# A perceiver block: routed experts with split down products, and one accumulator that the scatters add to one after the other

## The chip, the cores and the metric

One core of one Trainium2 chip runs the whole program. The metric is the device time of one execution in microseconds (us), the median of several runs.

## What is computed

The input has 8 x 64 = 512 tokens of 512 features. Three blocks follow, each added to its input: cross attention to a context, gated chunk attention with 16 heads, and a mixture of experts. The change touches the last one:

```python
def _moe(xf, gate_w, w1, w2, w3):
    ...
    h = silu(einsum('ecd,edi->eci', xb, w1)) * einsum('ecd,edi->eci', xb, w3)
    ob = einsum('eci,eid->ecd', h, w2)
    y_pairs = ob[buf_idx] * w_s[:, None]
    y = zeros((T, D)).at[t_s].add(y_pairs)          # T = 512 tokens, D = 512
shared = silu(xf @ sw1) * (xf @ sw3) @ sw2
x = x + (y + shared)                                # xf is the layer norm of x
```

Each token goes to 6 of 32 experts (inner width 352 = 128 + 128 + 96); the shared expert, twice as wide, sees all tokens. All arrays are fp32.

## The kernel before

The program is written engine by engine, with a semaphore for every dependency; nothing is scheduled by a tool. Each engine's block (`@block.sync`, `gpsimd`, `scalar`, `vector`, `tensor`) is executed in the order of its lines, and a waiting instruction holds everything behind it on its engine. SP issues the loads and stores, POOL (GpSimd) the indirect DMAs.

**Split products.** Where a product has to be exact but cheap, an fp32 matrix is cut in two fp32r halves: ScalarE copies it to the high half (`..._h`, `..._hi`), VectorE subtracts that to get the low half (`..._l`, `..._lo`), and TensorE makes three products (`mm3`, L316: high x high, high x low, low x high). What is not split is multiplied as plain fp32 in one instruction.

**Items.** A router on the chip sorts the token-expert pairs into items of up to 128 pairs of one expert. Item m has its list of tokens in a column of `tl` and its routing weights in `wl`. Its number decides the buffers: k = m % 2 for `xe`, `h`, `hT`, `ob`, and the PSUM banks. Turn i of the loops handles items 2i and 2i + 1. The eight steps of the shared expert (NSH = 8) run before item 0 and use the same functions.

**What each engine does in the turn of item m.**
- TensorE (`ex_pe`, L1024): transposes of item m + 1's tokens; the up products of item m (`ex_up`, 24 fp32r products of 352 columns, L318 to L320); the down product of item m - 1 (`ex_down`, L970, three fp32 products of 512 columns, L978); the transposes of item m's h (`ex_hT`, L963).
- ScalarE (`ex_act`, L1036): hT of item m - 1 out of PSUM (L1006, L1007), the high half of item m + 1's tokens (L1011), silu (L996), the high halves of item m + 1's w1 and w3 (`ex_act_w13`, L985, w_h<-w_raw, L988).
- VectorE (`ex_dve`, L1070): the low half of the tokens (L1015), copies of the token numbers for the next gather (`take`) and scatter (`give`), `ob` = down product x routing weight of item m - 2 (`ex_dve_ob`, L1053, L1061), h (L1001), the low halves of item m + 1's w1 and w3 (w_l<-w_raw,w_h, L992).
- POOL (`ex_pool`, L1108): the gather of item m + 3's tokens (L1094), then the scatter of item m - 2 (`ex_scatter`, L1097, L1098), which adds 128 rows of 2 KB to an accumulator in device memory. There are two accumulators, `y_scratch0` for even and `y_scratch1` for odd items, both zeroed early (L1251), so that two scatters in flight never touch the same bytes. `ob[k]` and `give[k]` are written again only when the scatter before it from the same k has landed (`acc_done[k]`, L1057).
- SP: the weights of an expert, once per expert (`cond=new`), up to four experts ahead, into four slots of `w13_raw` and `w2_raw` (`ex_load_w13`, L1139, waits for `w13_ready`; `ex_load_w2`, L1151, waits for `d_ps`).

**Slots of the halves.** w13_h and w13_l have two slots. The conversion for item m + 1 always goes to slot 1 - k. If item m is the second item of its expert, its up products read the slot of item m - 1, row `SLOT` of the list, and that is the slot which the conversion is about to overwrite; `ODD` then delays the conversion until item m's up products have ended:

```python
e.wait_ge(h3_ps, m + odd + NSH)
ex_act_w13(e, 1 - k, 0, i + (k + 2), raw)
```

**The end.** The last two items (34 and 35) are not scattered. TensorE multiplies `ob` with a one-hot matrix `home` (token x row) into PSUM, fp32 (L2087); SP reads both accumulators back, 1 MB each (L1315, L1317), each once the last scatter into it has landed; VectorE adds the first, the second and the PSUM banks to x, four tiles each (L1888, L1892, L1896), and SP stores tile by tile (L1320).

Of the kernel before, what the change touches and what calls it, by code (L numbers as in the profile page):

```python
# [24 lines left out]
ALU = mybir.AluOpType  # L25
ACT = mybir.ActivationFunctionType
AX = mybir.AxisListType
# [11 lines left out]
def perceiver_block(nc, x_in, ctx_in, ctxT_in, Wq, Wk, WkT, Wv, Wo, gq, gk,  # L39
# [17 lines left out]
    with stack:  # L57
# [129 lines left out]
        xe = sbuf(moe, "xe", [P, 2, D])  # L187
# [5 lines left out]
        ob = sbuf(moe, "ob", [P, 2, D])  # L193
# [4 lines left out]
        gateT = sbuf(moe, "gateT", [E, T])  # L198
# [5 lines left out]
        hots = sbuf(moe, "hots", [P, 2, TT * TOP_K * E])  # L204
        hot = hots[:, 0, :].rearrange("p (t k n) -> p t k n", t=TT, k=TOP_K)
        hotp = hots[:, 1, :].rearrange("p (t k n) -> p t k n", t=TT, k=TOP_K)
        home = hots[:, :, 0:T]
# [24 lines left out]
        EXPERT, LOADED, SLOT, ODD, FIRST, HELD = range(6)  # L232
        lst_f = sbuf(moe, "lst_f", [1, 6, ML + 1])
        lst_j = sbuf(moe, "lst_j", [1, ML + 1])
        lst = sbuf(moe, "lst", [1, 6, ML + 1], I32)
# [9 lines left out]
        y_back = [xn_c, w2_and_lists[:, 4 * W2:4 * W2 + TT * D].rearrange("p (t d) -> p t d", t=TT)]  # L245
# [4 lines left out]
        y_dram = [nc.dram_tensor(f"y_scratch{k}", [T + P, D], F32) for k in range(2)]  # L250
# [5 lines left out]
        ctxT_arrived = [sem(f"ctxT_arrived{g}") for g in range(5)]  # L256
# [14 lines left out]
        IO_RK, IO_SPARE, IO_TOKENS = 32, 80, 96  # L271
# [31 lines left out]
        y0_in, y1_in = sem("y0_in"), sem("y1_in")  # L303
        y_sum, out_ready, home_ready, last_ps = sem("y_sum"), sem("out_ready"), sem("home_ready"), sem("last_ps")
# [7 lines left out]
        hT_ps, hT_ready, d_ps = sem("hT_ps"), sem("hT_ready"), sem("d_ps")  # L312

# [286 lines left out]
        def xa_dve_scores(e, i, j):  # L600
# [9 lines left out]
            e.tensor_reduce(nmx[:, 0, bb], sc[:, bb, :], AX.X, ALU.max, negate=True).then_inc(mx_ready, 1)  # L610
            e.wait_ge(mx_ready, i * 4 + (j + 1))
            e.tensor_tensor(nmx[:, 1, bb], nmx[:, 0, bb], rq[:, bb], ALU.mult).then_inc(nmx_ready, 1)

        def xa_dve_norm(e, i, j):
            bb = slice(2 * j, 2 * j + 2)
            e.wait_ge(p_ready, i * 4 + (j + 1))
            e.reciprocal(rsm[:, bb], sm[:, bb]).then_inc(rsm_ready, 1)
            e.wait_ge(rsm_ready, i * 4 + (j + 1))
# [8 lines left out]
        def xa_dve_rq(e, p):  # L627
            e.wait_ge(rms_ready, p + 1)
            e.reciprocal(rq[:, :], rms[:, :]).then_inc(rq_ready, 1)
# [333 lines left out]
        def ex_hT(e, k, u):  # L963
            e.wait_ge(h_ready, u + 1)
            e.wait_ge(hT_ready, u)
# [4 lines left out]
        def ex_down(e, k, u, w, landed, bank_free=None):  # L970
# [8 lines left out]
            m.then_inc(d_ps, 1)  # L979

# [27 lines left out]

        def ex_act_xT(e, m, k):
# [14 lines left out]
        def ex_pe(e, i, k, first=False, last=False):  # L1024
# [6 lines left out]
            ex_up(lambda c: xeT_h[:, k, c, :], lambda c: xeT_l[:, k, c, :], k, item_value(e, SLOT, m), m * 2 + 6)  # L1031
            ex_down(e, 1 - k, m + (NSH - 1), 1 if first else item_value(e, FIRST, m - 1, 3),
# [3 lines left out]
        def ex_act(e, i, k, last=False):  # L1036
# [3 lines left out]
            if last:  # L1040
                ex_act_silu(e, k, m + NSH)
                return
# [1100 lines left out]
```

## Time and profile before

| | |
|---|---|
| median of 3 runs | 1017.85 us (1016.35 to 1021.34) |
| the profiled execution | 1024.46 us, its span 1022.7 us |
| busy in the span | TensorE 97%, its weight loads 81%, VectorE 65%, ScalarE 53%, POOL 24% |
| first up product of item 0 / of item 35 | 735.7 us / 999.9 us into the span |
| DMA | 144.03 MB, mean 141 GB/s over the span |

The span runs from the first to the last instruction of the core; the execution's own time holds what lies around it too. The rows further down are from the same profiled execution. Matmuls overlap: their pace is read from start to start, not from the duration of one.

### The profile page before, as it was taken

How to read it: one execution, taken by the hardware profiler on the slowest of the kernel's cores; microseconds unless marked ns; L12 is line 12 of the kernel's file. 1: busy time of each engine (PE TensorE's matmuls, PEld its weight loads, DVE VectorE, ACT ScalarE, POOL GpSimd, SP SyncE). 2: the span in 40 equal slices, each digit the busy share in tenths (PEclk: the TensorE clock that was granted, in tenths of full speed). 3: DMA queues.
4: the chain of work that ended last, by engine and by line, in shares of the span. 5: the costliest groups of instructions: out<-in, count | busy, mean ns of one | idle time of the engine just before them, and what ended most of it. 6: DMA issues, size and time to landing. Idle time of an engine off the chain costs nothing.

```text
span 1022.7 us, 18723 instructions
## 1 busy us (share of the span) xinstructions
PE 993.1 (97%) x5468; PEld 828.9 (81%) x5469; DVE 669.1 (65%) x1022; ACT 541.0 (53%) x894; POOL 246.4 (24%) x170
## 2 busy tenths in 40 slices
PE   8899899999999999999999999989999999999997
PEld 7788698889898987888888888777777777777874
DVE  5655655675567665667787675667566677666765
ACT  6444575657566666554555543541356555545551
POOL 2200221323032152223333300010123343334331
PEclk9899999999999998999999999999999999999999
DMA  9100353321331331122221106211678889998995
GB/s 312 48 0 1 82 201 104 103 58 45 102 103 51 85 114 63 61 83 82 82 82 62 41 21 232 63 42 49 232 206 267 268 284 310 345 313 283 282 323 149
DMA packets 75567, 144.03 MB, mean 141 GB/s; under 512 B 13476, under 2 KB 40996, under 8 KB 75280
## 3 DMA queue, kind: packets, MB, share of 16 engines
q1 hardware_dynamic: 67680, 131.48, 38.4%
q0 software_dynamic: 7856, 12.16, 5.7%
q8 instruction: 17, 0.28, 0.1%
q14 instruction: 14, 0.11, 0.0%
HBM read 146.86 MB, written 14.02 MB: 157 GB/s over the span
## 4 chain that ended last, share of the span: by engine, by line
PE 74%; SPq 6%; DMA 6%; DVE 6%; issue 5%; ACT 4%; DVEq 0%; ACTq 0%
PE ps L318 19%; PE ps L319 18%; PE ps L320 18%; PE ps L710 6%; PE ps L978 6%; DMA w_raw<-in_w 4%; SPq L945 2%; PE ps L777 1%; PE ps L787 1%; SPq L1119 1%; PE ps L767 1%; DMA wo_raw<-in_owT 1%; DVE w_l L992 1%; ACT wo_h L406 1%; PE ps L697 1%
## 5 line engine op out<-in xcount | busy, mean ns | idle before, releaser
L992 DVE TENSOR_TENSOR w_l<-w_raw,w_h 128x1408 fp32r<-128x1408 f32 x76 | 121.8, 1625 | 37.9 <-ACT w_h L988 25.8
L988 ACT ACTIVATE w_h<-w_raw 128x1408 fp32r (+1 forms) x76 | 102.6, 1373 | 54.7 <-DMA w_raw<-in_w 39.2
L978 PE MATMUL ps<-w_and_lists,hT 128*128 (+3 forms) x264 | 121.5, 596 | 0.0
L739 POOL TENSOR_TENSOR lw_l<-lw_raw,lw_h 128x1024 fp32r<-128x1024 f32 x32 | 77.0, 2411 | 145.8 <-ACT lw_h L735 140.5
L318 PE MATMUL ps<-w_h,xeT_h 128*128 x288 | 97.4, 338 | 5.4 <-DVE w_l L992 4.6
L319 PE MATMUL ps<-w_l,xeT_h 128*128 x288 | 93.1, 323 | 0.0
L320 PE MATMUL ps<-w_h,xeT_l 128*128 x288 | 93.0, 323 | 0.0
L1094 POOL DMA_INDIRECT xe<-xn_scratch,take x37 | 39.4, 1066 | 220.1 <-DVE ob L1061 148.3
L978 PEld LDWEIGHTS ps<-w_and_lists,hT 128*128 128x128 f32 (+1 forms) x264 | 47.9, 189 | 44.0 <-issue 43.0
L318 PE MATMUL ps<-xT_hi,lw_h 128*128 128x512 f32 x192 | 78.3, 408 | 0.0
L319 PE MATMUL ps<-xT_lo,lw_h 128*128 128x512 f32 x192 | 77.3, 403 | 0.0
L320 PE MATMUL ps<-xT_hi,lw_l 128*128 128x512 f32 x192 | 76.4, 398 | 0.0
L1564 DVE TENSOR_REDUCE ssk<-sqk 128x4 f32<-128x512 f32 (+1 forms) x64 | 43.6, 685 | 36.8 <-ACT sqk L1409 36.6
L1409 ACT ACTIVATE sqk<-ps 128x512 f32<-128x512 f32 x64 | 38.1, 597 | 47.2 <-PE ps L320 42.2
L318 PEld LDWEIGHTS ps<-w_h,xeT_h 128*128 128x128 f32 x288 | 54.4, 189 | 10.4 <-issue 10.1
L710 PE MATMUL ps<-pT,ctx 128*128 128x128 f32 x512 | 62.1, 277 | 0.6 <-ACT pT L582 0.3
L710 PEld LDWEIGHTS ps<-pT,ctx 128*128 128x128 f32 x512 | 59.1, 192 | 2.2 <-ACT pT L582 2.2
L1098 POOL DMA_INDIRECT y_scratch<-ob,give x34 | 55.5, 1631 | 21.4 <-DVE ob L1061 11.6
L592 POOL TENSOR_TENSOR wq_l<-wq_raw,wq_h 128x1024 fp32r<-128x1024 f32 x8 | 19.3, 2410 | 170.0 <-ACT wq_h L552 170.0
L883 DVE RECIPROCAL q_r<-q_r 128x512 f32<-128x512 f32 x16 | 53.6, 3347 | 6.0 <-ACT q_r L859 6.0
L318 PE MATMUL ps<-wk_h,cT_h 128*128 128x512 f32 (+1 forms) x128 | 52.2, 408 | 4.3 <-DVE ssk L1564 2.6
L319 PEld LDWEIGHTS ps<-w_l,xeT_h 128*128 128x128 f32 x288 | 54.2, 188 | 0.0
(315 smaller groups left out, 2543.8 us busy)
## 6 DMA issues: line engine op xcount, KB each, us to landing
w_raw<-in_w SPq DMA_DIRECT2D x78, 704.0 KB
w_and_lists<-in_w SPq DMA_DIRECT2D x39, 512.0 KB
w_and_lists<-in_w SPq DMA_DIRECT2D x39, 192.0 KB
rkB<-rk_scratch SPq DMA_DIRECT2D x56, 128.0 KB, 3.2
wq_raw<-in_Wq SPq DMA_DIRECT2D x8, 512.0 KB, 4.6
wo_raw<-in_Wo SPq DMA_DIRECT2D x16, 256.0 KB, 2.8
lw_raw<-in_kwT SPq DMA_DIRECT2D x8, 512.0 KB, 3.3
lw_raw<-in_qwT SPq DMA_DIRECT2D x8, 512.0 KB, 3.4
```

The costliest lines, as they stand in the source:

```text
L318: nc.tensor.matmul(out_ap, lh, rh, start=first, stop=False)
L319: nc.tensor.matmul(out_ap, lh, rl, start=False, stop=False)
L320: return nc.tensor.matmul(out_ap, ll, rh, start=False, stop=last)
L710: m = e.matmul(ps[:, 4 + j % 2, at:at + P], ctx[:, b * KPB + t, hcol(c)], pT[:, b, t, :], start=t == 0, stop=t == KPB - 1)
L739: e.tensor_tensor(lw_l[n][:, :, :], lw_raw[n][:, :, :], lw_h[n][:, :, :], ALU.subtract).then_inc(lw_ready[n], 1)
L883: e.reciprocal(q_r[:, k, :], q_r[:, k, :]).then_inc(q_recip, 1)
L978: m = e.matmul(ps[:, 6 + k, :], hT[r, k, c, :], w2_raw[r, slot(w), c, :], start=c == 0, stop=c == FC - 1)
L988: e.activation(w13_h[:, k, n, :, :], w13_raw[:, slot(raw), n, :, :], ACT.Copy).then_inc(w13_hi_s, 1)
L992: e.tensor_tensor(w13_l[:, k, n, :, :], w13_raw[:, slot(raw), n, :, :], w13_h[:, k, n, :, :], ALU.subtract).then_inc(w13_ready, 1)
L1094: e.indirect_dma_start(xe[:, k, :], None, xn_dram.ap(), bass.IndirectOffsetOnAxis(ap=take[:, k:k + 1], axis=0), bounds_check=T - 1, oob_is ...
L1098: e.indirect_dma_start(y_dram[k].ap(), bass.IndirectOffsetOnAxis(ap=give[:, k:k + 1], axis=0), ob[:, k, :], None, bounds_check=T - 1, oob_ ...
L1564: e.tensor_reduce(ssk[:, t, bass.ds(g * 4, 4)], sqk[:, t % 2, :].rearrange("p (h n) -> p h n", n=P), AX.X, ALU.add).then_inc(sqk_free, 1)
```

## The change

Five edits, four in the routed experts and one in the way their results are added up. The items stay the same, in the same order.

1. The down product of a routed item: its two whole chunks of 128 are split into halves, hT (`hT_h`, `hT_l`) and w2 (into `xT_hi`, `xT_lo`, which are free by then); six fp32r products take the place of two fp32 ones, the third chunk of 96 stays fp32. The shared expert's down stays as it was.
2. `ob` is written by ScalarE instead of VectorE.
3. Each item uses its own slot k of w13_h and w13_l; `SLOT` and `ODD` are gone, and the conversion waits for h3_ps of item m - 1 in all cases.
4. At the end, `home` and `ob` are fp32r (`ob_h`, `ob_l`), two products for each tile and item in the place of one.
5. One accumulator `y_scratch`. It isn't zeroed: SP writes x with the shared expert's part into it (waiting for d_read = 8), so that the last step adds only the read-back and PSUM, tile by tile. POOL holds each scatter until the one of the item before has landed, and the first until x has.

Core of the diff (names of buffers, semaphore renames and the attention's `soft_step`, which replaces three semaphores by one in the same places, are left out):

```diff
+        def ex_down_halves(e, m, k, w):
+            e.wait_ge(hT_ready, m * 2 + (NSH + 2))
+            e.wait_ge(d_read, m + (NSH - 1))
+            e.wait_ge(w2_ready, m + 1)
+            for c in range(FC - 1):
+                mm3(ps[:, 6 + k, :], hT_h[:, k, c, :], hT_l[:, k, c, :], xT_hi[:, 2 * k + c, :], xT_lo[:, 2 * k + c, :],
+                    c == 0, False)
+            r = slice(0, FW[-1])
+            e.matmul(ps[:, 6 + k, :], hT[r, k, FC - 1, :], w2_raw[r, slot(w), FC - 1, :], start=False, stop=True).then_inc(d_ps, 1)
...
+        def ex_dve_hT_low(e, m, k):
+            e.wait_ge(hT_ready, m * 2 + (NSH + 1))
+            e.tensor_tensor(hT_l[:, k, :, :].rearrange("p c n -> p (c n)"), ps[:, 5, 0:(FC - 1) * P],
+                            hT_h[:, k, :, :].rearrange("p c n -> p (c n)"), ALU.subtract).then_inc(hT_ready, 1)
+
+        def ex_act_w2(e, i, k, raw):
+            e.wait_ge(w2_in[k], i * 32 + 64)
+            e.activation(xT_hi[:, 2 * k:2 * k + 2, :], w2_raw[:, slot(raw), 0:FC - 1, :], ACT.Copy).then_inc(w2_hi_s, 1)
+
+        def ex_dve_w2(e, m, k, raw):
+            e.wait_ge(w2_hi_s, m + 1)
+            e.tensor_tensor(xT_lo[:, 2 * k:2 * k + 2, :], w2_raw[:, slot(raw), 0:FC - 1, :], xT_hi[:, 2 * k:2 * k + 2, :],
+                            ALU.subtract).then_inc(w2_ready, 1)
+
+        def ex_act_ob(e, i, k, out=ob):
+            m = i * 2 + k
+            if not isinstance(i, int) or i > 0:
+                e.wait_ge(acc_done[k], i * 16)
+            e.wait_ge(d_ps, m + (NSH + 1))
+            e.activation(out[:, k, :], ps[:, 6 + k, :], ACT.Copy, scale=wl[:, bass.ds(m, 1)]).then_inc(d_read, 1)
...
-            e.wait_ge(h3_ps, m + odd + NSH)
-            ex_act_w13(e, 1 - k, 0, i + (k + 2), raw)
-            ex_act_w13(e, 1 - k, 1, i + (k + 2), raw)
...
+            if not last and (not isinstance(m, int) or m > 0):
+                e.wait_ge(h3_ps, m + NSH)
+                ex_act_w13(e, 1 - k, 0, i + (k + 2), raw)
+                ex_act_w13(e, 1 - k, 1, i + (k + 2), raw)
+            ex_act_w2(e, i, k, own)
...
         def ex_scatter(e, k):
-            e.indirect_dma_start(y_dram[k].ap(), bass.IndirectOffsetOnAxis(ap=give[:, k:k + 1], axis=0), ob[:, k, :], None,
+            e.indirect_dma_start(y_dram.ap(), bass.IndirectOffsetOnAxis(ap=give[:, k:k + 1], axis=0), ob[:, k, :], None,
                                  bounds_check=T - 1, oob_is_err=False, compute_op=ALU.add).then_inc(acc_done[k], 16)
...
             e.wait_ge(d_read, i * 2 + (k + NSH + 1))
             e.sem_inc(acc_turn, 1)
+            if not isinstance(i, int) or i * 2 + k > 0:
+                e.wait_ge(acc_done[1 - k], i * 16 + k * 16)
+                e.sem_inc(acc_turn, 1)
             ex_scatter(e, k)
...
-            for k in range(2):
-                e.dma_start(y_dram[k].ap().rearrange("(t p) d -> p t d", p=P),
-                            zeros[:, :].unsqueeze(1).to_broadcast([P, TT + 1, D])).then_inc(scratch_io, 16)
...
-            for m in (2, 3, 4):
+            for m in (2, 3):
                 ex_load_w13(e, m, m % 2, m // 2 + 1, values[m])
             for m in (1, 2, 3):
                 ex_load_w2(e, m, m % 2, m // 2 + 1, values[m])
+            ex_load_w13(e, 4, 0, 3, values[4])
+            e.wait_ge(d_read, NSH)
+            e.dma_start(y_dram.ap()[0:T, :].rearrange("(t p) d -> p t d", p=P), x[:, :, :]).then_inc(scratch_io, 16)
...
             for m in range(4):
+                if m == 2:
+                    e.wait_ge(scratch_io, IO_X)
                 ex_pool(e, m // 2, m % 2)
...
-                return e.matmul(ps[:, t, :], home[:, k, t * P:(t + 1) * P], ob[:, k, :], start=k == 0, stop=k == 1)
+                one = home[:, k, t * P:(t + 1) * P]
+                e.matmul(ps[:, t, :], one, ob_h[:, k, :], start=k == 0, stop=False)
+                return e.matmul(ps[:, t, :], one, ob_l[:, k, :], start=False, stop=k == 1)
```

The order of three engines in the loop body, as the built programs have it (the changed program's lines are shifted, L327 is `mm3`'s first product there, L318 here).

TensorE, the down product of the item before, between the last up product and the transposes of h. Before:

```order
L978 ISA
L978 MATMUL ps<-w_and_lists,hT 128x512
L964 REGISTER_ALU
L967 MATMUL ps<-ident,h 128x128 x2
L967 MATMUL ps<-ident,h 96x128
```

and changed, where the first three products stand twice:

```order
L327 MATMUL ps<-xT_hi,hT_h 128x512
L328 MATMUL ps<-xT_lo,hT_h 128x512
L329 MATMUL ps<-xT_hi,hT_l 128x512
L999 ISA
L999 MATMUL ps<-w_and_lists,hT 128x512
L973 REGISTER_ALU
L976 MATMUL ps<-ident,h 128x128 x2
L976 MATMUL ps<-ident,h 96x128
```

L978 stands three times before; now it is L999, once, behind six products on halves. The place in the order is the same.

VectorE, one item from h to the next h. Before (the second item of a turn):

```order
L1001 TENSOR_TENSOR h<-h,ps 128x352
L992 TENSOR_TENSOR w_l<-w_raw,w_h 128x1408
L1015 TENSOR_TENSOR xeT_l<-ps,xeT_h 128x512
L1091 COPY take<-tl 128x1
L1059 COPY give<-tl 128x1
L1061 TENSOR_SCALAR ob<-ps,wl 128x512
```

and changed:

```order
L1021 TENSOR_TENSOR h<-h,ps 128x352
L1012 TENSOR_TENSOR w_l<-w_raw,w_h 128x1408
L1048 TENSOR_TENSOR xT_lo<-w_and_lists,xT_hi 128x1024
L1038 TENSOR_TENSOR hT_l<-ps,hT_h 128x256
L1065 TENSOR_TENSOR xeT_l<-ps,xeT_h 128x512
L1165 COPY take<-tl 128x1
L1116 COPY give<-tl 128x1
```

The product for w_l stands twice in both. Two low halves have come in behind it, ob has gone to ScalarE, where it stands between xeT_h and silu; w2's high half stands there behind the two of w_h.

POOL, the first item of a turn of the loop, with what each waits for. Before:

```order
L1112 REGISTER_ALU [waits xeT_ps]
L1094 DMA xe<-xn_scratch,take 128x512 [waits take_ready]
L1104 REGISTER_ALU [waits give_ready]
L1098 DMA y_scratch<-ob,give 640x512 [waits d_read]
```

and changed:

```order
L1189 REGISTER_ALU [waits xeT_ps]
L1168 DMA xe<-xn_scratch,take 128x512 [waits take_ready]
L1178 REGISTER_ALU [waits give_ready]
L1181 REGISTER_ALU [waits d_read]
L1172 DMA y_scratch<-ob,give 640x512 [waits acc_done1]
```

The order of gather and scatter is the same; the scatter has one wait more, for the landing of the scatter from the other slot.

## Rows read from the trace of the kernel before

**Rows 1.** Windows of the items; columns in the first row.

```profile
core 0: us, PE busy (x) PEld busy (x) DVE busy (x) ACT busy (x) POOL busy (x), PEclk, DMA share, GB/s
735.70:832.20 96.50, 95.53 (x482) 75.82 (x482) 63.36 (x88) 51.45 (x75) 33.16 (x25) 1.00 0.81 250
832.20:883.90 51.70, 51.45 (x261) 40.62 (x261) 35.66 (x49) 29.14 (x42) 19.43 (x15) 1.00 1.00 325
883.90:924.60 40.70, 38.33 (x189) 29.04 (x187) 25.76 (x35) 21.30 (x32) 13.19 (x10) 1.00 0.92 303
924.60:999.90 75.30, 73.56 (x368) 57.55 (x367) 51.67 (x70) 41.70 (x60) 25.30 (x19) 1.00 0.93 299
```

**Rows 2.** Timeline of PE over one item: start us, us, engine line op.

```profile
865.80 2.74 PE L978 MATMUL ps<-w_and_lists,hT 128*128 x6
868.38 0.50 PE L967 MATMUL ps<-ident,h 128*128 128x128 f32 x3
...
869.12 0.41 PE L318 MATMUL ps<-w_h,xeT_h 128*128 x1
...
876.35 0.41 PE L318 MATMUL ps<-w_h,xeT_h 128*128 x1
```

**Rows 3.** Timeline of PE in the attention stage, fp32r products of 512 columns.

```profile
599.97 0.39 PE L318 MATMUL ps<-xT_hi,lw_h 128*128 128x512 f32 x1
600.20 0.40 PE L319 MATMUL ps<-xT_lo,lw_h 128*128 128x512 f32 x1
```

**Rows 4.** Waits, 760 to 1000 us: us in total, times, longest.

```profile
ACT w_h L988 <- DMA w_raw<-in_w: 39.2, 30, 2.3
```

**Rows 5.** Groups by form, whole span: busy us, mean ns of one, idle before.

```profile
L1061 DVE TENSOR_SCALAR ob<-ps,wl 128x512 f32<-128x512 f32 x36 | 26.7, 742 | 6.5 <-PE ps L978 6.5
...
L1560 DVE TENSOR_TENSOR cT_l<-ctxT,cT_h 128x1024 fp32r<-128x1024 f32 x3 | 3.7, 1226 | 1.1 <-ACT cT_h L1399 1.1
...
L449 DVE TENSOR_TENSOR ao_l<-ps,ao_h 128x256 fp32r<-128x256 f32 x4 | 1.7, 414 | 0.4 <-ACT ao_h L444 0.4
...
L735 ACT ACTIVATE lw_h<-lw_raw 128x1024 fp32r<-128x1024 f32 x32 | 33.6, 1052 | 10.8 <-PE ps L320 10.8
...
L1011 ACT ACTIVATE xeT_h<-ps 128x512 fp32r<-128x512 f32 x36 | 21.5, 596 | 22.3 <-issue 20.6 <-PE ps L1021 1.7
```

**Rows 6.** Timeline of VectorE between two items.

```profile
866.08 0.52 DVE L1001 TENSOR_TENSOR h<-h,ps 128x352 f32<-128x352 f32 x1 [1.07 <-PE ps L320]
...
867.02 1.63 DVE L992 TENSOR_TENSOR w_l<-w_raw,w_h 128x1408 fp32r<-128x1408 f32 x1 [0.42 <-issue]
...
868.96 1.63 DVE L992 TENSOR_TENSOR w_l<-w_raw,w_h 128x1408 fp32r<-128x1408 f32 x1 [0.32 <-ACT w_h L988]
```

**Rows 7.** Timeline of POOL, a gather and the scatter behind it.

```profile
865.14 1.05 POOL L1094 DMA_INDIRECT xe<-xn_scratch,take  x1 [4.55 <-DVE ob L1061]
...
866.49 1.59 POOL L1098 DMA_INDIRECT y_scratch<-ob,give  x1 [0.30 <-issue]
```

**Rows 8.** Software queue, windows 870:872.2, 872.2:873.8, 873.8:875.4: packets, MB, engines' share.

```profile
q0 software_dynamic: 95, 0.17, 30.6%
...
q0 software_dynamic: 69, 0.11, 36.3%
...
q0 software_dynamic: 28, 0.04, 12.8%
```

**Rows 9.** Timeline from item 34's down product to the end.

```profile
1004.03 2.84 PE L978 MATMUL ps<-w_and_lists,hT 128*128 x6
...
1004.18 1.55 POOL L1098 DMA_INDIRECT y_scratch<-ob,give  x1 [5.60 <-DVE ob L1061]
...
1008.93 0.40 SPq L1317 DMA_DIRECT2D w_and_lists<-y_scratch  x1
...
1011.63 6.17 PE L2087 MATMUL ps<-ob,hots 128*128 128x512 f32 x14
...
1017.49 2.47 DVE L1896 TENSOR_TENSOR x<-x,ps 128x512 f32<-128x512 f32 x4
```

More of the change, by code:

```diff
@@ L197, in perceiver_block @@
         gw_l = sbuf(moe, "gw_l", [P, DC, E], F32R)
-        gateT = sbuf(moe, "gateT", [E, T])
+        with ExitStack() as router_rows:
+            gateT = sbuf(router_rows, "gateT", [E, T])
+        hT_l = sbuf(moe, "hT_l", [P, 2, FC - 1, P], F32R)
         gate = sbuf(moe, "gate", [P, TT, E])
@@ L1068, in ex_dve_x, with homes, ex_dve_ob_low, ex_dve @@
             e.tensor_tensor(x[:, u % TT, :], x[:, u % TT, :], ps[:, 6 + u % 2, :], ALU.add).then_inc(d_read, 1)
[L1070 removed]
+        def homes(e, i):
+            e.wait_ge(pool_consts, 10)
+            for k in range(2):
+                e.tensor_scalar(home[:, k, :], iota_t[:, :], tl_f[:, 1, bass.ds(i * 2 + k, 1)], None,
+                                ALU.is_equal).then_inc(home_ready, 1)
+        def ex_dve_ob_low(e, i, k):
+            m = i * 2 + k
+            e.wait_ge(d_read, m + (NSH + 1))
+            e.scalar_tensor_tensor(ob_l[:, k, :], ps[:, 6 + k, :], wl[:, bass.ds(m, 1)], ob_h[:, k, :], ALU.mult,
+                                   ALU.subtract).then_inc(home_ready, 1)
+        def ex_dve(e, i, k, own, ahead=None, last=False):
             m = i * 2 + k
             if last:
[L1074 to L1078 removed]
+                ex_dve_give(e, ahead, k)
+            if not isinstance(m, int) or m > 0:
+                ex_dve_hT_low(e, m - 1, 1 - k)
+            if last:
+                homes(e, i)
+            if not last:
+                ex_dve_xT(e, m + 1, 1 - k)
+                ex_dve_take(e, m + 3, 1 - k)
             if isinstance(i, int) and i == 0:
                 ex_dve_x(e, NSH - 2 + k)
[L1081 to L1082 removed]
+            elif not last:
+                ex_dve_give(e, i - 1 if ahead is None else ahead, k)
             ex_dve_h(e, k, m + NSH)
[L1084 to L1085 removed]
+            raw = None if last else raw_slot(e, m + 1)
+            if not last and (not isinstance(m, int) or m > 0):
                 ex_dve_w13(e, 1 - k, 0, m * 2 + 7, raw)
                 ex_dve_w13(e, 1 - k, 1, m * 2 + 8, raw)
+            ex_dve_w2(e, m, k, own)
+            return raw
         def ex_dve_take(e, m, k):
@@ L1545, in _ @@
             ex_act_xT(e, 0, 0)
-            ex_act(e, 0, 0)
-            ex_act(e, 0, 1)
-            with e.Fori(1, last_act) as i:
-                ex_act(e, i, 0)
-                ex_act(e, i, 1)
-            ex_act(e, last_act, 0)
-            ex_act(e, last_act, 1, last=True)
-            ex_act_hT(e, 1, last_act * 2 + (NSH + 1))
+            raw = ex_act(e, 0, 0, 0)
+            raw = ex_act(e, 0, 1, raw)
+            raw = ex_act(e, 1, 0, raw)
+            ex_act(e, 1, 1, raw)
+            with e.Fori(2, last_act) as i:
+                raw = ex_act(e, i, 0, raw_slot(e, i * 2))
+                ex_act(e, i, 1, raw)
+            ahead_act = turn_ahead(e)
+            raw = ex_act(e, last_act, 0, raw_slot(e, last_act * 2), ahead_act)
+            ex_act(e, last_act, 1, raw, ahead_act, last=True)
+            ex_act_hT_halves(e, last_act * 2 + 1, 1)
+            for k in range(2):
+                ex_act_ob(e, last_act, k, ob_h)
         @block.vector
```

169 lines of the change are left out of this document (81 added, 88 removed).

## The prediction

> **What bounds the kernel now.** The change touches the last quarter: 36 items of up to 128 tokens each, for 32 experts. I read the windows first [rows 1], cut where items 0, 13, 20, 25 and 35 start their first product (13, 7, 5 and 10 periods). The reader is to see two things. TensorE is busy for 258.87 of 264.2 us, so it looks like the bound, at the granted clock 1.00 (2.4 GHz) throughout. But the DMA share is 0.81, then 1.00, 0.92, 0.93. The periods are 96.5/13 = 7.42, 51.7/7 = 7.39, 40.7/5 = 8.14 and 75.3/10 = 7.53 us. The PE timeline [rows 2] gives TensorE's own period: 869.12 to 876.35 = 7.24 us, of which the down projection takes 865.80 to 868.38 = 2.58 us and the two groups of transposes 0.74, so the up products take the other 3.9. A new expert brings 2 x 128 x 1408 x 4 + 128 x 1024 x 4 + 96 x 512 x 4 bytes = 2.16 MB, gather and scatter 0.52 MB more. At the 325 GB/s of the second window 2.69 MB take 8.3 us. So the stage is bound by TensorE while it has loads in hand, and by the DMA once these are used up: the third window is such a stretch. The waits say the same: ScalarE waits 39.2 us in all, in 30 pieces, for w_raw to land [rows 4].
>
> **Down projection in halves.** Today three fp32 products run as six passes, 0.43 us apart (2.58/6). Two of the three become three fp32r products each; these follow one another at 0.23 us for 512 columns [rows 3]. New: 6 x 0.23 + 0.86 = 2.24 us, a gain of 0.34 per item, 11.6 us over the 34 downs that run before item 35's up products end. The Trainium skill (FP8 and Floating Point Precision, section TensorE Precision Notes) says that true FP32 makes four passes: four of 0.23 would be 0.92 per chunk, the gain 0.46 per item and 15.6 in all. The trace has 0.86, and the sum goes by it.
>
> **Its price on the other engines.** VectorE gets a low half of 128x1024 (1.23) and one of 128x256 (0.41) and loses ob (0.74): +0.90. ScalarE gets a high half of 128x1024 (1.05) and ob (about 0.60, like xeT_h from PSUM): +1.65 [rows 5]. In the second window VectorE is busy 35.66/7 = 5.09 per item and ScalarE 29.14/7 = 4.16, so 6.0 and 5.8 of a period of 6.9: nothing as sums. The tight spot is the handover [rows 6]: h at 866.08, w_l from 867.02, done at 868.65. TensorE starts the next item at 869.12 and would want it at 868.78. The second w_l ends at 870.59, and TensorE wants it half of the up products (1.9 us) after its start, at 870.7. Both still fit, by 0.1 us; I take nothing, with 0.1 to 0.3 us per item as the bad end (up to 10 us).
>
> **Own slot for each item.** The second item of an expert no longer makes the next conversion wait for h3_ps + odd. Four experts have two items (36 against 32); a late conversion shows as a period of about 7.59 instead of 7.24, so 0.35 each, 1.4 at most, about 1.0 where the DMA isn't behind.
>
> **What the DMA takes back.** In the first window the DMA share is 0.81, so the gain can show: 13 x 0.34 + 1.0 = 5.4. Over the other 22 periods a faster TensorE only asks sooner. The room there is the idle share, 0.08 x 40.7 + 0.07 x 75.3 = 8.5 us, while TensorE would offer 7.1. Since the stalls come earlier once the reserve is drained faster, I take little of it: 1.5, between 0 and 7.1.
>
> **x into the accumulator.** SP now waits for d_read = 8 (the shared half of all tiles is in x), then writes 1 MB, ahead of item 5's weights; behind that wait stand the loads of items 5 and up. The load of item 4 moves behind three w2 loads. 1.05 MB at 325 GB/s is 3.2 us, in the least loaded window: between 0 and 3.2, I take 1. The two writes of zeros go; they lie far ahead, beside attention: nothing. Three one-partition list steps go: I take nothing.
>
> **The chained scatters.** POOL now issues a scatter only when the one before has landed; behind the wait stands the next gather, and ScalarE's ob and VectorE's give wait for the scatter two back. The trace of before shows no such wait, so I bound the landing. The last scatter, alone, starts at 1004.18, and SP, which waits for it, issues at 1008.93: 4.75 us [rows 9]. The one at 866.49 [rows 7] shares the DMA with weights: the software queue carries 30.6% until 872.2, 36.3% until 873.8, 12.8% until 875.4 [rows 8], which I read as gather first, scatter behind it, landed by 875.4: 8.9 us. The next scatter starts one period (7.24) later, 1.7 us before that. So the wait is real wherever weights stream. But the 8.9 us hold the gather's transfer, issued 1.35 us ahead of it (865.14): a scatter held back while the gather runs has less in front of it. From one landing to the next the queue then needs about the 7 us that it needs today. I expect POOL to slip some 2 us behind, once, and then keep the pace; each ob slot has a whole period to spare. Cost: 0 to 12, I take 1.
>
> **The tail.** From item 34's down (1004.03) to the end (1022.7) are 18.7 us [rows 9]. New, from the start of that down: 2.24 + 0.34; item 35's hT split on ScalarE and VectorE, about 1.35; its down 2.24 (6.2). The four products of k = 0 take 8 x 0.23 = 1.84 beside the split of ob, so k = 1 runs from 8.1, a tile each 0.46; 14 passes take 6.17 us today. Of the additions four remain instead of twelve. The last result would be ready at about 10.8, and from the end of today's last additions (1017.49 + 2.47 = 1019.96) to the end of the span are 2.7: 13.5 us. The other branch is the read-back, 1 MB now, not 2: scatter 33 must first see scatter 32 land. If it starts where it starts today and lands 4.75 later, the four reads come at about +10.5, and the end at +14. Gain 4.5, between 2 and 5.2.
>
> **Sum.** -5.4 - 1.5 + 1 + 1 - 4.5 = -9.4, rounded with the three list steps to -9.9. The profiled execution took 1024.46 us (span 1022.7), 0.65% above the median 1017.85 of the runs shown; the difference of 9.9 goes on the median: 1008 us.
>
> **The rivals.**
> DMA takes it all in the loop: the second window with its share of 1.00 speaks for it, the 0.81 of the first against it. Only the tail stays, less the x write: 1014.
> TensorE's pace holds throughout (all room of the DMA is used): 11.6 + 1.4 + 5.2 = 18: 1000. The third window speaks against it.
> The chain of scatters becomes the bound. If a scatter beside weights needs 8.9 us from its start even with nothing of its queue ahead, the chain runs at 9.0 per item against 7.6 (167.7/22) in the last 22 periods: 31 us. One period is covered by the second ob slot, and since waiting items let the weights run ahead, which frees the DMA for the scatters, I count half of the rest, 12; the tail gives back 4.5. That is +7.5, 1025. It decides as soon as the landing beside weights stays over about 7.6 us. For it: the software queue has only 13 to 36% of the engines [rows 8], which is how a queue looks that gets turns beside a bigger one. Against it: the gather in front. The Trainium skill (DMA: Bandwidth & Descriptors, section Queues, rings and completion order) says that each DMA engine takes turns between the queues that have work, a packet at a time; by that rule, holding the scatters back makes a lone one no faster beside weights, and this rival's time holds. Its section Anatomy of one DMA puts such a transfer at about 2.0 us plus bytes over 436 GB/s, 2.6 us here, by which the chain would never bind; the 4.75 and 8.9 of the trace speak against that figure.
>
> **How the numbers follow.** Forecast 0.48, DMA takes it all 0.20, TensorE's pace 0.12, scatter chain 0.20. A measurement of this kernel tells about 0.5%, 5 us, from no change: below 1012.8 is faster, above 1022.9 slower. Faster: 0.46 + 0.12 + 0.04 = 0.62; within: 0.20; slower: 0.18. The range of 1000 to 1023 leaves out the far ends of the last two rivals.
>
> **What would show it.** Right: six passes of the down become six fp32r products and two passes, 2.24 us; periods near 6.9 in the first 13 items and still 8 us in some stretch behind the 19th item; the conversions held by w_raw landing, for 39 us or more in all; POOL idle before the scatter, now for a landing, 1 to 3 us each, without ScalarE's ob waiting for anything but TensorE; 14 us from item 34's down to the end. Wrong: ScalarE's ob or VectorE's give idle for a landing (the chain binds, and the DMA share falls under 0.9); TensorE waiting for w2's low half or for hT_l; periods of 7.2 and more in the first 13 items, which would mean that VectorE has become the bound.

## The result and the profile after

| | before | changed |
|---|---|---|
| median of 6 runs | 1017.63 us | 1038.34 us |
| range of the runs | 1016.16 to 1021.34 us | 1032.62 to 1043.48 us |
| the profiled execution | 1024.46 us, span 1022.7 us | 1034.06 us, span 1032.3 us |

The ratio is 1.0192, 95% interval 1.0157 to 1.0226: the change costs about 20 us. The prediction said 1008 us, 1000 to 1023. The time lies outside its range, on the other side of no change.

The windows of the changed kernel, cut at the same items as [rows 1] (0, 13, 20, 25, 35), and below them all 35 periods in one:

```profile
core 0: us, PE busy (x) PEld busy (x) DVE busy (x) ACT busy (x) POOL busy (x), PEclk, DMA share, GB/s
732.00:830.20 98.20, 93.43 (x508) 81.74 (x507) 75.24 (x102) 69.58 (x100) 35.00 (x24) 0.98 0.84 269
830.20:883.30 53.10, 51.02 (x276) 44.89 (x275) 39.11 (x56) 38.48 (x54) 22.70 (x14) 0.97 0.92 307
883.30:928.50 45.20, 38.60 (x196) 32.34 (x196) 29.80 (x41) 27.85 (x43) 19.90 (x11) 0.96 0.84 269
928.50:1012.40 83.90, 73.63 (x389) 63.18 (x388) 59.19 (x81) 54.79 (x81) 36.81 (x19) 0.98 0.82 261
...
732.00:1012.40 280.40, 256.68 (x1362) 222.16 (x1361) 203.34 (x277) 190.69 (x275) 114.40 (x67) 0.98 0.85 274
```

The 35 periods took 264.2 us before and take 280.4 now: +1.7, +1.4, +4.5 and +8.6 us in the four windows. Ahead of item 0 the changed execution is 3.7 us shorter (732.0 against 735.7) and behind item 35's start 2.9 (19.9 against 22.8), so the two profiled spans differ by 9.6 us, and the loss lies in the periods. The medians differ by 20.7 us. The profiled execution of before was 6.8 us over its median and that of the changed kernel 4.3 under, so a comparison of windows with before understates what the change costs; where the two disagree, the ratio of the runs counts. No engine is full any more: TensorE was busy for 258.87 of 264.2 us, now for 256.68 of 280.4, the DMA share fell from 1.00, 0.92, 0.93 to 0.92, 0.84, 0.82 in the last three, and VectorE and ScalarE have 77 and 90 us of room. A stage that becomes slower while nothing in it is full may be waiting for a latency. The waits from 760 us to the end of the loop name it (us in total, times, longest):

```profile
POOL y_scratch L1172 <- DMA y_scratch<-ob,give: 113.1, 27, 7.0
ACT ob L1057 <- DMA y_scratch<-ob,give: 59.4, 23, 4.8
...
DVE give L1116 <- DMA y_scratch<-ob,give: 19.6, 12, 2.4
...
PE ps L327 <- DVE w_l L1012: 13.2, 13, 1.3
...
ACT w_h L1008 <- DMA w_raw<-in_w: 4.6, 6, 1.1
```

The wait for weights, 39.2 us before [rows 4], is down to 4.6: weights now lie ready and wait for the loop. In its place stand three waits for the landing of a scatter. Their effect inside a period, from the timeline (start us, us, operation, in brackets the idle time before it and what ended it):

```profile
898.31 0.15 DVE L1116 COPY give<-tl 128x1 int32 x1 [2.27 <-DMA y_scratch<-ob,give]
898.38 0.69 ACT L1057 ACTIVATE ob<-ps,wl 128x512 f32<-128x512 f32 x1 [4.64 <-DMA y_scratch<-ob,give]
...
899.05 1.59 POOL L1172 DMA_INDIRECT y_scratch<-ob,give  x1 [5.75 <-DMA y_scratch<-ob,give]
...
900.10 0.61 PE L976 MATMUL ps<-ident,h 128*128 128x128 f32 x3 [1.31 <-DVE h L1021]
...
900.95 2.42 POOL L1168 DMA_INDIRECT xe<-xn_scratch,take  x1 [0.31 <-issue]
...
902.50 0.66 PE L327 MATMUL ps<-w_h,xeT_h 128*128 128x352 f32 x1 [1.07 <-DVE w_l L1012]
```

ScalarE's ob waits for its slot, that is for the scatter two back. Behind ob stand silu and the conversions of the next item's weights, behind give stands h. TensorE has nothing until h comes (1.31 us), and is idle again (1.07) until the late w_l is there. The chain of waits over the same stretch (start us, us, what):

```profile
879.84 8.27 DMA y_scratch<-ob,give
...
888.98 9.20 DMA y_scratch<-ob,give
...
899.05 9.31 DMA y_scratch<-ob,give
```

From each landing to the next scatter's start there is 0.9 us (888.98 + 9.20 = 898.18, and the next starts at 899.05), in POOL's own instructions. Each scatter has nothing of its kind in front, and still takes 8.3 to 9.3 us. These are the signs that the prediction named for being wrong: ob and give idle for a landing, and a DMA share under 0.9 (0.92, 0.84 and 0.82 in the last three windows).

### The profile page after: what moved, and what is told of

Its sections match the earlier page's. It is cut to its first block, busy times and chain, and to the rows that moved or that the text cites. A ratio compares the mean times of both kernels' runs of the same rounds, so it can differ in the third digit from the quotient of the medians.

```text
span 1032.3 us, 18416 instructions
## 1 busy us (share of the span) xinstructions
PE 982.0 (95%) x5540; PEld 844.7 (82%) x5541; DVE 691.1 (67%) x1049; ACT 590.8 (57%) x966; POOL 271.3 (26%) x170
## 4 chain that ended last, share of the span: by engine, by line
PE 63%; DMA 25%; issue 4%; DVE 4%; ACT 4%; POOLq 0%; SPq 0%; ACTq 0%; DVEq 0%
DMA y_scratch<-ob,give 23%; PE ps L327 16%; PE ps L328 16%; PE ps L329 16%; PE ps L719 6%; PE ps L987 2%; PE ps L796 1%; PE ps L786 1%; PE ps L776 1%; DMA wo_raw<-in_owT 1%; ACT wo_h L415 1%; PE ps L706 1%; PE ps L2119 1%; DMA ctxT<-in_ctxT_in 0%; PE ps L769 0%
## 5 line engine op out<-in xcount | busy, mean ns | idle before, releaser
L327 PE MATMUL ps<-w_h,xeT_h 128*128 128x352 f32 x288 | 99.0, 344 | 13.4 <-DVE w_l L1012 13.4
L328 PE MATMUL ps<-w_l,xeT_h 128*128 128x352 f32 x288 | 95.7, 332 | 0.0
L329 PE MATMUL ps<-w_h,xeT_l 128*128 128x352 f32 x288 | 95.5, 332 | 0.0
L1172 POOL DMA_INDIRECT y_scratch<-ob,give x34 | 58.2, 1713 | 138.5 <-DMA y_scratch<-ob,give 121.1
L1168 POOL DMA_INDIRECT xe<-xn_scratch,take x37 | 61.6, 1664 | 96.0 <-DVE take L1165 62.2
L327 PE MATMUL ps<-xT_hi,lw_h 128*128 128x512 f32 x192 | 77.4, 403 | 0.0
L327 PEld LDWEIGHTS ps<-w_h,xeT_h 128*128 128x128 f32 x288 | 56.7, 197 | 16.6 <-DVE w_l L1012 16.5
L1057 ACT ACTIVATE ob<-ps,wl 128x512 f32<-128x512 f32 x34 | 23.3, 687 | 59.8 <-DMA y_scratch<-ob,give 59.7
L328 PEld LDWEIGHTS ps<-w_l,xeT_h 128*128 128x128 f32 x288 | 56.4, 196 | 0.0
L329 PEld LDWEIGHTS ps<-w_h,xeT_l 128*128 128x128 f32 x288 | 56.3, 195 | 0.0
L327 PE MATMUL ps<-wk_h,cT_h 128*128 128x512 f32 (+1 forms) x128 | 51.7, 404 | 4.5 <-DVE ssk L1651 2.6
```

The costliest lines, as they stand in the source:

```text
L327: nc.tensor.matmul(out_ap, lh, rh, start=first, stop=False)
L328: nc.tensor.matmul(out_ap, lh, rl, start=False, stop=False)
L329: return nc.tensor.matmul(out_ap, ll, rh, start=False, stop=last)
L1168: e.indirect_dma_start(xe[:, k, :], None, xn_dram.ap(), bass.IndirectOffsetOnAxis(ap=take[:, k:k + 1], axis=0), bounds_check=T - 1, oob_is ...
L1172: e.indirect_dma_start(y_dram.ap(), bass.IndirectOffsetOnAxis(ap=give[:, k:k + 1], axis=0), ob[:, k, :], None, bounds_check=T - 1, oob_is_ ...
```

## The experiments

Where an experiment's 35 periods are given, they run from the first product of item 0 to that of item 35, in a window of its profiled execution. Before it is 264.2 us (in an execution 6.8 us over the median), changed 280.4. The ratios are to the kernel before as it ran beside each experiment; its median lay between 1017.35 and 1020.41 us, so ratios and not medians are compared between experiments. e3, e5 and e6 are single runs.

**e1: the changed kernel without the chain.** Two accumulators again, the rest of the change stays.

```
-        y_dram = nc.dram_tensor("y_scratch", [T + P, D], F32)
+        y_dram = [nc.dram_tensor(f"y_scratch{k}", [T + P, D], F32) for k in range(2)]
...
             e.sem_inc(acc_turn, 1)
-            if not isinstance(i, int) or i * 2 + k > 0:
-                e.wait_ge(acc_done[1 - k], i * 16 + k * 16)
-                e.sem_inc(acc_turn, 1)
             ex_scatter(e, k)
...
+            for t in range(TT):
...
+                e.tensor_tensor(x[:, t, :], x[:, t, :], y_back[1][:, t, :], ALU.add).then_inc(out_ready, 1)
```

(x is written to the first accumulator, zeros to the second; at the end both are read back, as before the change.)

> The changed kernel with two accumulators again and without the wait for the scatter ahead; everything else of the change stays (down halves, slots, ob on ScalarE, x in the accumulator, tail). Theory, the chain of landings binds: POOL no longer waits for a landing, ScalarE's ob and VectorE's give wait for nothing but TensorE, periods 6.9 in the first 13 items, the 35 periods together about 256 to 262 us instead of 280, and the whole about 1008 us (1003 to 1013). Rival, another part of the change costs the time (the two-input operations on VectorE, the write of x, the conversions): 1030 us or more, with periods of 8 us and more still there in the first 20 items.

Measured: 1008.75 us median, 0.9908 of before (0.9884 to 0.9932). The periods and three waits, 732 to 1000 us:

```profile
735.30:988.80 253.50, 247.40 (x1362) 216.85 (x1361) 203.12 (x276) 191.61 (x273) 116.32 (x68) 0.99 0.92 303
```

```profile
ACT w_h L1008 <- DMA w_raw<-in_w: 30.8, 31, 1.5
...
ACT ob L1057 <- DMA y_scratch<-ob,give: 4.0, 6, 0.9
PE ps L327 <- DVE w_l L1012: 2.9, 11, 0.5
```

So everything but the chain and the single buffer makes the kernel faster, by about 9 us, and those two cost about 29 us. TensorE's busy time is 11.5 us under that of before, as the halves were to give. The landing itself is no shorter here, 9.1 us in the median of the stretch from 874 to 924 us; with two scatters in flight POOL never waits for it, and ob only for 4.0 us in all.

**e2: the kernel before with the chain alone.** The three lines that e1 takes out, put into the kernel before.

> The kernel before with one thing added: a scatter waits until the one ahead of it has landed. Two accumulators, six passes, everything else as before. Theory, the chain of landings binds: it runs at about 10 us per item beside weights against a period of 7.24, so stretches with periods of 9 to 10 us appear, and the time is 12 to 30 us over the kernel before, 1030 to 1047 us. Rival, the wait costs only because TensorE is faster or because all scatters go to one buffer: within 5 us of before.

Measured: 1036.08 us, 1.0189 (1.0169 to 1.0209), 19 us more than before.

```profile
731.20:1008.20 277.00, 263.58 (x1291) 205.33 (x1291) 177.17 (x242) 142.79 (x206) 99.68 (x67) 0.99 0.85 273
```

The wait alone does it, at TensorE's old pace and with two buffers. The chain brings both kernels to nearly the same loop, 277.0 and 280.4 us, and to the same step from scatter to scatter: 8.04 us on average here (31 steps, 766.01 to 1015.23), 7.98 in the changed kernel. A chain of landings does not care how fast TensorE is.

**e4: two accumulators, the chain kept.** e1 with the wait of the changed kernel.

> The changed kernel with two accumulators, but the wait for the scatter ahead kept. Theory, the wait binds and not the buffer: landings of 8 to 9.5 us beside weights as in the changed kernel, and its time within 5 us (1033 to 1044 us). Rival, additions that fall into one buffer slow each other: the landings get shorter and the time falls by 10 us or more, towards 1010 to 1020 us.

Measured: 1041.2 us, 1.0243 (1.0204 to 1.0282), loop 283.2 us. The scatters from 868 to 922 us take 8.1 to 9.0 us to land. The buffer is not the cause; the wait is. From e1 to e4 the three lines of the wait are the only difference, and both ran beside the same runs of before: from 0.9908 to 1.0243, or from 1008.75 to 1041.2 us, the wait alone costs 32 to 34 us on the kernel with halves.

**e3: few weights.** The changed kernel; from the seventh item on nothing is loaded, and the items multiply by what lies in the slots (this part of the computation is changed).

```
+                step(e.memset(lst[0:1, LOADED, 6:ML], 0))
```

> The changed kernel, but from the seventh item on no expert's weights are loaded (the computation then uses weights that lie in the slots already, so this part of the computation is changed). Theory, the landing is long because the scatter shares the DMA engines with weights: the landing falls to 4.6 to 5.5 us, POOL waits for none, all periods are 6.9 to 7.0, and the 35 periods take about 243 us instead of 280, the whole about 1000 us. Rival, the landing is long because a gather or another scatter of the same queue is in front: it stays at 7 us or more, and periods of 8 us and more remain.

Measured, one run: 1001.06 us, all periods from item 4 on 6.8 to 6.9 us (6.82 to 6.91), the loop 245.5 us. The DMA's view of the stretch from 874 to 924 us, with the median from issue to landing at the end; first the changed kernel:

```profile
q1 hardware_dynamic: 3153, 12.39, 69.6%
...
y_scratch<-ob,give POOLq DMA_INDIRECT x6, 8.1
```

and with few weights:

```profile
q0 software_dynamic: 1571, 2.50, 29.1%
...
xe<-xn_scratch,take POOLq DMA_INDIRECT x8, 3.3
y_scratch<-ob,give POOLq DMA_INDIRECT x7, 5.6
```

The same scatter, with the same gather beside it: 5.6 us instead of 8 to 9. Of that, 2.5 us are POOL's issue, which took 1.6 us in the changed kernel, so behind the issue 3.1 us are left of some 7. With 5.6 us the chain has room in a period of 6.91. POOL still waited four times, 14.5 us in all, in the first items, where weights were loading.

**e5: small gathers.** The changed kernel; in POOL's turns from item 4 on, which gather the tokens of item 7 and up, a gather fetches 16 of its 128 rows (this part of the computation is changed).

```
+            e.indirect_dma_start(xe[0:n, k, :], None, xn_dram.ap(), bass.IndirectOffsetOnAxis(ap=take[0:n, k:k + 1], axis=0),
```

> The changed kernel (one accumulator, chain), but from item 4 on a gather fetches only the first 16 of its 128 rows (the other rows are an earlier item's, so this part of the computation is changed). Theory, a scatter beside weights is slow through the weights and not through the gather: landings of 7.5 to 9 us stay, POOL still waits over 80 us in all, 1025 us or more. Rival, the gather's rows, issued right behind the scatter, take the software queue's turns: landings fall to 6 us or less, the periods to about 7, and the time to 1010 to 1015 us.

Measured, one run: 1019.0 us, loop 262.3. The chain of waits, links from 879 to 906 us:

```profile
879.00 6.08 DMA y_scratch<-ob,give
...
885.94 6.28 DMA y_scratch<-ob,give
...
893.09 6.04 DMA y_scratch<-ob,give
...
899.99 6.09 DMA y_scratch<-ob,give
```

Neither theory had it right. The landing falls from 8.3 to 9.3 us to 6.1 in this stretch, so the gather has a share of some 3 us in it; but elsewhere it stays (9.0 us from 966.0 to 975.0). Over all 33 steps of the chain the average step falls only from 7.98 to 7.46 us (757.51 to 1003.67). POOL still waits for 128.6 us in all, and the time lies between the two forecasts.

**e6: a plain scatter.** The changed kernel; the scatter overwrites and doesn't add (this part of the computation is changed).

```
-                                 bounds_check=T - 1, oob_is_err=False, compute_op=ALU.add).then_inc(acc_done[k], 16)
+                                 bounds_check=T - 1, oob_is_err=False).then_inc(acc_done[k], 16)
```

> The changed kernel with the chain, but the scatter overwrites instead of adding (this part of the computation is changed). Theory, the landing is long because its packets take turns with the weights' and not because of the addition: landings shorten by 1 us at most, the time stays at 1028 us or more. Rival, the reading and adding at the far end makes the landing long: it falls to 6 us or less, POOL's waits go, and the time is 1010 to 1018 us.

Measured, one run: 1012.99 us, loop 257.5.

```profile
884.30 7.08 DMA y_scratch<-ob,give
...
892.25 7.16 DMA y_scratch<-ob,give
...
900.27 6.99 DMA y_scratch<-ob,give
```

My theory failed here: I allowed the addition 1 us, and it is 2 us of the landing beside weights (0.6 of them in POOL's issue, 1.59 us with the addition and 1.02 without). The rival had the time, but not all of the way: the landing did not fall to 6 us, and POOL still waits for 84.9 us in all. The price depends on the load: the shortest landings of the two kernels are 4.24 and 4.60 us, only 0.4 apart. With 7.0 and the 0.9 between, the chain runs at 7.9 per item, and that is what the weights allow in this stretch anyway (the periods of e1 there are 7.1 to 8.1). Two microseconds of nine decide over some 25 us, by this one run.

**e7: the wait for x behind the gather.** e1, where item 3's period had been 10.4 us: POOL waited 11.6 us for x to land in the accumulator, with a gather behind that wait. It is the gather of item 5's tokens, which TensorE transposes right before item 4's products (the expectation calls it item 4's).

```
             for m in range(4):
-                if m == 2:
-                    e.wait_ge(scratch_io, IO_X)
...
             ex_gather(e, 1 - k)
+            if isinstance(i, int) and m == 2:
+                e.wait_ge(scratch_io, IO_X)
```

> The kernel e1 (two accumulators, no chain) with one more edit: POOL waits for x to land in the accumulator behind item 4's gather instead of ahead of it. In e1 that gather was issued at 757.7 us, 11.6 us idle before it, and the period of item 3 was 10.4 us instead of 6.9. Theory, the write of x costs through the gather behind its wait: that period falls to 6.9 to 7.5, and the time by 2.5 to 3.5 us, to about 1005.5 us. Rival, the load of item 4 behind the write is what is late, or the lost time is waited for by the DMA anyway: within 1.5 us of e1, with another wait at the same place.

Measured: 1010.32 us, 0.9893 (0.9864 to 0.9923). Item 3's period is 6.96 us, but the loop takes 253.3 us against 253.5: 3.0 us are won up to item 13 (91.5 against 94.5) and 2.8 lost behind it; over the periods ScalarE's wait for weights and TensorE's for w_l grow by 2 us each. The second half of the rival had it. e1, e7 and e10 can't be told from each other; they are the fastest here with the whole computation, about 1% under before and 3% under the changed kernel.

**e8: six passes again.** e1 with the down projection in six passes, as before. Its first two chunks use an hT that isn't the item's (that part of the computation is left out); all conversions stay.

```
-                mm3(ps[:, 6 + k, :], hT_h[:, k, c, :], hT_l[:, k, c, :], xT_hi[:, 2 * k + c, :], xT_lo[:, 2 * k + c, :],
-                    c == 0, False)
+                e.matmul(ps[:, 6 + k, :], hT[:, k, c, :], w2_raw[:, slot(w), c, :], start=c == 0, stop=False)
```

> The kernel e1 with the down projection as six fp32 passes again; its hT of the first two chunks is not the items' (that part of the computation is left out), and all conversions, ob on ScalarE and the slots stay. Theory, the halves are worth their full 0.34 us per item, also behind item 13, because the DMA still has room: periods of 7.24 undisturbed, and 9 to 12 us over e1, 1018 to 1021 us. Rival, the DMA takes the gain back in the last 22 periods, as I predicted: only 5 to 6 us over e1, about 1014 us.

Measured: 1011.38 us, 0.9919 (0.9889 to 0.9949).

```profile
730.20:986.80 256.60, 255.39 (x1294) 202.59 (x1293) 203.14 (x277) 192.72 (x274) 120.91 (x68) 1.00 0.91 299
```

TensorE is busy 8.0 us longer than in e1, and the loop is 3.1 us longer; idle time of TensorE is 1.2 us here and 6.1 in e1. Of these 6.1, 2.9 are the wait for the late gather of item 5, so e7 is the better measure: there the loop is 3.3 us shorter than here (2.6 up to item 13, 0.7 behind it), and TensorE is idle for 5.5 us, 5.0 of them until w_l comes. More than half of the halves' gain in busy time goes into waiting for weights. By the ratios they are worth 1 to 3 us, with intervals as wide as that. Both forecasts were too high.

**e9: own slots alone, on the kernel before.**

```
-            ex_up(lambda c: xeT_h[:, k, c, :], lambda c: xeT_l[:, k, c, :], k, item_value(e, SLOT, m), m * 2 + 6)
+            ex_up(lambda c: xeT_h[:, k, c, :], lambda c: xeT_l[:, k, c, :], k, k, m * 2 + 6)
...
-            e.wait_ge(h3_ps, m + odd + NSH)
+            e.wait_ge(h3_ps, m + NSH)
```

> The kernel before with one part of the change alone: each item uses its own slot of the converted halves, and the conversion never waits for the up products of the same expert's first item. The kernel e8, which has six passes as before and no chain, still ran 9 us ahead of before, and its 35 periods took 256.6 us against 264.2, so something other than the halves gave some 7 us in the loop. Theory A, it is this slot: stalls behind the four second items go, the loop takes about 258 us, and the time falls by 4 to 7 us. Theory B, my predicted size holds (0.35 us per second item): 1 us or nothing that can be told, and the gain of e8 lies in the other parts (ob on ScalarE, the order of the loads, the tail).

Measured: 1016.63 us, 0.9973 (0.9953 to 0.9994), so 2.8 us less than before, 0.6 to 4.8. The loop is 259.3 us. My 1.0 us lies inside the interval, 4 to 7 for the most part outside it. The 7 us between e8's loop and that of before, from which Theory A was made, come in part from the slow profiled execution of before.

**e10: ob back on VectorE.** e7 with the weighting on VectorE.

```
-            if not isinstance(m, int) or m >= 2:
-                ex_act_ob(e, i - 1 if ahead is None else ahead, k)
...
+            e.tensor_scalar(ob[:, k, :], ps[:, 6 + k, :], wl[:, bass.ds(m, 1)], None, ALU.mult).then_inc(d_read, 1)
```

> The kernel e7 (two accumulators, no chain, the wait for x behind the gather) with the weighting ob on VectorE again, as before the change (0.74 us there). Theory A, ob on ScalarE gives nothing by itself, but VectorE then has no room: w_l ends 0.7 us later, TensorE waits for it, undisturbed periods of 7.2 to 7.6 instead of 6.91, and 8 to 12 us over e7, near 1020 us. Theory B, VectorE still has the room: periods of 6.91 stay and the time is within 3 us of e7.

Measured: 1009.15 us, 0.9885 (0.9861 to 0.9909); undisturbed periods of 6.91 us.

```profile
736.40:988.70 252.30, 247.56 (x1363) 215.88 (x1361) 222.88 (x310) 173.69 (x241) 115.27 (x68) 1.00 0.92 304
```

Theory B: VectorE is busy 6.37 us per item and has room in 6.91. Moving ob to ScalarE gives nothing that can be told; it isn't needed for the halves either.

## Why the prediction was wrong

**The step that failed is the chained scatters**, priced at 1 us between 0 and 12. It was priced so by two sentences: "a scatter held back while the gather runs has less in front of it", and "From one landing to the next the queue then needs about the 7 us that it needs today". Measured, the wait costs 19 us on the kernel before (e2) and 32 to 34 on the kernel with halves (e4 against e1), and the step is 8.0 us on average. The first two points are what was wrong in this term, the third is about the rival that had it right.

1. The landing. I read 8.9 us for a scatter behind its gather [rows 7, 8] and took the gather out of it. The runs show that in the stretch around 890 us the gather has some 3 us in it (e5), the addition 2 (e6), and that the weights are needed for most of it (e3: 5.6 us with gather and addition but without weights). But holding the scatter back doesn't take the gather away. POOL issues the next gather right behind the scatter, at 900.95 behind 899.05 in the timeline above, and its rows then fall beside the scatter instead of ahead of it.
2. The 0.9 us from a landing to the next issue, which no term had. From the first scatter of the changed kernel to the last the chain never breaks:

```profile
755.90 1.63 POOL L1172 DMA_INDIRECT y_scratch<-ob,give  x1 [0.30 <-issue]
```

```profile
1019.21 1.55 POOL L1172 DMA_INDIRECT y_scratch<-ob,give  x1 [3.90 <-DMA y_scratch<-ob,give]
```

263.3 us for 33 steps are 7.98 per item, an average that holds landings of 4.6 to 9.8 us. The rival's threshold, "the landing beside weights stays over about 7.6 us", should have been landing plus 0.9 against the period that the loop could otherwise keep, which is 253.5/35 = 7.24 us in e1. The mean landing, 7.1 us, is under my threshold, and the chain binds all the same.
3. The rival. "The chain becomes the bound" had the mechanism and the place. Its rate of 9.0 us per item for the last 22 periods was too high: they took 182.2 us, 8.28 each. That is 14.5 us over before in the profiled executions, where the rival counted 31 and then took 12, since waiting items let weights run ahead; the landings of 4.6 us are in line with that, and the discount was sound as far as these executions tell. What it left out are the first 13 periods, where chain and buffer cost 3.7 us against e1. Why its 1025 us is 13 too low stays open beyond that: in the profiled executions the whole difference is 9.6 us against its 7.5, by the medians it is 20.7, and no run tells in which periods the rest lies. The rival got 0.20; the rows had a landing of 8.9 us that overlapped the next scatter by 1.7 us, and with them it deserved more.

The rule of the Trainium skill that I cited against my forecast (DMA: Bandwidth & Descriptors, section Queues, rings and completion order: an engine takes turns between queues with work) gave this outcome, and e3 agrees with it: without the weights in the other queue the scatter lands in 5.6 us instead of 8 to 9. Of the 3 us in e5 it says nothing, since gather and scatter go through the same software queue. An estimate by the page's formula for one transfer (section Anatomy of one DMA), 2.6 us here, is far from every landing seen, counted from the start of the issue: 4.6 to 4.8 us alone, 5.6 with few weights.

**The other terms**, against e1 and the parts of it:

- Halves of the down projection. The price was right: from the first of the six products to the transposes behind are 2.25 us (predicted 2.24), and undisturbed periods are 6.91 us (6.9):

```profile
1016.36 0.39 PE L327 MATMUL ps<-xT_hi,hT_h 128*128 128x512 f32 x1
...
1018.61 0.50 PE L976 MATMUL ps<-ident,h 128*128 128x128 f32 x3
```

- What the DMA takes back. I let 4.4 us of the halves stand in the first 13 items and 1.5 in the rest. Between e8 and e7 the loop differs by 2.6 us in the first 13 and 0.7 in the rest, so more was taken back in both. That a faster start drains the reserve of weights earlier is my explanation; TensorE's waits for w_l, 1.0 us in e8 and 5.0 in e7, are in line with it.
- Own slots: 1.0 predicted, 2.8 measured (e9), with an interval of 0.6 to 4.8 that holds the 1.0.
- x into the accumulator: 1 predicted. Not the 1 MB on the DMA but the gather behind POOL's wait cost something: item 3's period was 8.9 us in the changed kernel, 10.4 in e1, and 7.3 in e8 with the same wait. e7 takes that away (6.96) and the total doesn't move, so its net price is about nothing.
- VectorE's and ScalarE's load at nothing: right. e10 adds even 0.7 us per item to VectorE and loses nothing that can be told.
- The tail. Predicted 18.7 to 14 us; it is 15.9 us (1016.36 to 1032.3). The read-back branch sets it, as the text had it, but scatter 33 doesn't start "where it starts today". It stands in the chain: its issue comes 2.85 us behind the down product's start (1019.21), not 0.15. From there:

```profile
1024.04 1.79 SPq L1397 DMA_DIRECT2D w_and_lists<-y_scratch  x4
1024.15 0.69 ACT L1057 ACTIVATE ob_h<-ps,wl 128x512 fp32r<-128x512 f32 x1 [3.89 <-DMA y_scratch<-ob,give]
...
1026.80 1.35 DVE L1972 TENSOR_TENSOR x<-w_and_lists,ps 128x512 f32<-128x512 f32 x2 [1.00 <-DMA w_and_lists<-y_scratch]
```

Even item 35's ob_h waits for that landing, though TensorE's down product had ended a microsecond and more before.

The terms without the chain added up to -10.4 us, -10.9 with the 0.5 that the sum took for three list steps although their own term gave them nothing. e1 measures -9.4, with the halves smaller than forecast, the slots perhaps larger, and the tail 2.0 us better instead of 4.5 (from item 35's first product to the end: 1022.7 - 999.9 = 22.8 before, 1009.6 - 988.8 = 20.8 in e1, which still reads two accumulators back; 19.9 in the changed kernel). That the total comes near the forecast is luck in part: the terms erred in both directions. With 1 to 3 us for the halves, 2.8 for the slots and 2.0 for the tail, some 2 to 4 us of e1's gain are not assigned: the order of the loads around item 4 and the writes of zeros were not tried alone.

## What to carry to other kernels

Where a change makes each transfer wait for the landing of the one before, the stage gets a floor: items times (landing plus the hop to the next issue). Take the landing as it is with everything that shares the engines, and don't take out what is merely moved behind it. Its average lies between the landing alone and the one under full load (here 4.6 and 9.8, mean 7.1 us), since stalls let the other transfers run ahead; already the mean plus the hop of 0.9 was over the 7.24 us that the stage would have without the wait. Set the sum against that period; two buffers with two transfers in flight hide the very same landing. When a stage gets slower while every engine and the DMA get emptier, look for such a latency chain.

## What was not expected of the hardware

- Behind some short idles TensorE runs at its lower clock. After the idles of 1.31 and 1.07 us around 900 us the granted clock was 0.52 over the next 3.1 us, which is the lower level (1.2 GHz) for nearly all of them, and the up products stood 0.29 us apart (902.97 to 903.26) instead of 0.16 (892.71 to 892.87):

```profile
888.00:902.50 14.50, 10.45 (x52) 7.80 (x50) 8.31 (x12) 9.55 (x13) 7.16 (x4) 0.99 1.04 342
902.50:905.60 3.10, 3.10 (x11) 3.10 (x12) 3.10 (x4) 1.31 (x4) 0.87 (x1) 0.52 0.97 278
```

```profile
902.97 0.49 PE L328 MATMUL ps<-w_l,xeT_h 128*128 128x352 f32 x1
903.26 0.49 PE L329 MATMUL ps<-w_h,xeT_l 128*128 128x352 f32 x1
```

  Half of such a stretch is lost, an estimate of some 1.5 us from the two spacings. The trace shows it several times in the loop (a granted clock of 0.98 over it, 1.00 before), and not behind every idle of that length: the one of 1.31 us that ended at 892.44 is followed by full clock. What decides between the two is not shown.
- The addition in a scatter is not free beside weights: 2 us of a landing of 9 (e6), 0.6 of them in POOL's issue, which takes 1.59 us with it, 1.02 without. Between the shortest landings, 4.60 and 4.24 us, it makes 0.4. The Trainium skill (DMA: Bandwidth & Descriptors, section SDMA does more than copy) places the adder in the data stream and states no price for it.
- POOL's issue of a gather took 1.05 us [rows 7] and takes 2.42 us at 900.95, when VectorE works on w_l from two inputs in SBUF (from 900.83 on). The scatter's issue goes from 1.6 to 2.5 us in the same way where it starts beside w_l (e3). The Trainium skill (GPSIMD Engine Reference, section Specifications) says that the two engines share their SBUF interfaces, with contention where a VectorE instruction has two SBUF inputs; these rows agree. Not every overlap lengthens an issue: the scatter at 866.49 [rows 7] took 1.59 us, though w_l ran from 867.02 on [rows 6]. For the gathers this cost nothing here, since POOL waited anyway. A longer issue of a scatter (2.47 us at 792.97) is part of its landing, and so of the chain.
